# ScalarE copies a finished layer's rows straight into the PSUM factor, in place of the DMAs that spread them and one wide copy

## Chip, cores and metric

The kernel runs on one core of a Trainium2 chip. The metric is the device time of one execution in microseconds; less is better. TensorE (PE) multiplies, VectorE (DVE) forms products and remainders, ScalarE (ACT) rounds, copies and applies the activation, GpSimd (POOL) forms remainders, and SyncE's queue (SP) issues the DMAs.

## What is computed

A compressed interaction network over 512 samples with 32 fields and 16 embedding dimensions. Each of three layers multiplies every row of its input with every one of the 32 field rows and contracts the products with a weight matrix:

```python
def _cin(x0, conv_params, split_flags):
    B, _, D = x0.shape
    x = x0
    results = []
    for (W, b), split in zip(conv_params, split_flags):
        h = x.shape[1]
        z = jnp.einsum('bhd,bmd->bhmd', x, x0).reshape(B, h * x0.shape[1], D)
        xk = jax.nn.relu(jnp.einsum('oc,bcd->bod', W, z) + b[None, :, None])
        if split:
            half = xk.shape[1] // 2
            x, xk = (xk[:, :half], xk[:, half:])
        else:
            x = xk
        results.append(xk)
    return jnp.sum(jnp.concatenate(results, axis=1), axis=2)
pooled = _cin(sparse_embed, [(W1, b1), (W2, b2), (W3, b3)], [True, True, False])
return pooled @ Wo.T + bo
```

Each layer has 128 output rows. Layers 1 and 2 hand 64 of them on as the next layer's x; the other 64, and all of layer 3, are results. Everything is float32.

## The kernel before

**Tiling.** The 512 x 16 = 8192 columns are cut into 16 chunks of 512 columns. Layer 1 of a chunk is one group of 4 product tiles of 128 x 512 and a quarter tile; layers 2 and 3 are four groups of 4 tiles each. A pass i of the program works on layer 1 of chunk i (group 0 of the pass), layer 2 of chunk i-1 (groups 1 to 4) and layer 3 of chunk i-2 (groups 5 to 8), in this order on every engine. Passes run from 0 to 17; passes 0, 1, 16 and 17 hold fewer groups, and passes 4 to 13 are a loop. The first three groups (pass 0, and groups 0 and 1 of pass 1) are "native": no rounding, all matmuls in plain fp32.

**One group.** DVE multiplies a factor with the field rows and writes product tiles `z` (`product`, L533). ACT rounds them to `zh` (L423). POOL forms the remainder `zl` = `z` - `zh` (L481); in groups 0, 1, 3, 5 and 7 one tile goes another way: DVE writes it to PSUM (`zx_ps`), ACT rounds it (L427), and DVE subtracts (L594). PE multiplies `zh` (L682, L684, L690), the native tiles (L694), and last `zl` (L700, L706), into the layer's accumulator `y_ps`. Groups 2, 4, 6 and 8 give POOL three tiles (1536 columns), the others two (1024). The z buffers form a ring of three: a product waits until PE is through with the group three before (`group_used`).

**The factor.** In layers 2 and 3 the factor of a group is `a_ps[:, half, :]`, in PSUM: half 0 for the layer's first two groups, half 1 for the last two. It holds the 64 rows of the finished layer's x in blocks of 32 partitions: rows 0-31, 32-63, 0-31, 32-63 in half 0, and 32-63, 0-31, 32-63, 0-31 in half 1. ACT writes x to SBUF as `x_out[layer]` (L391, partitions 0-63 for layer 1 and 64-127 for layer 2), SP's queue copies it with five DMAs (`spread`, L323; two for half 0, three for half 1) into `a_rep`, and ACT copies each half, 128 x 512, to `a_ps` (`a_to_psum`, L378). The native group 1 of pass 1 reads `a_rep` itself.

**Order on ACT.** After the zh of a group ACT does other work written at that place in `body` (L414): at group 0 the copy for layer 2's half 1; at group 3 that for layer 3's half 0 and layer 3's result (`y_to_sbuf(3)`); at group 4 `y_to_sbuf(1)`, that is x (L391) and result (L399, partitions 64-127) of layer 1; at group 5 the copy for layer 3's half 1 and then `x_to_psum` (L375), the factor of the next pass's layer 1; at group 7 the copy for layer 2's half 0 and `y_to_sbuf(2)`. The queue is in order: a zh waits for what stands before it.

**Order on SP.** One queue issues all DMAs. In pass i: the spread of layer 1's x, once it exists; (pass 0) the rest of the first `b_fac`, the field rows that layers 2 and 3 multiply with, and the second part of layer 2's weights; (pass 1) layer 3's weights; the field rows of chunk i+2 (`load_x`, 1.5 MB); the spread of layer 2's x; `b_fac` of chunk i+1 (2 MB).

Of the kernel before, what the change touches and what calls it, by code (L numbers as in the profile page):

```python
# [44 lines left out]
P = 128  # L45
Q = 32
# [3 lines left out]
CH = 512  # L50
# [3 lines left out]
HALF = 64  # L54
# [85 lines left out]
def i_is(i, number):  # L140

    return isinstance(i, int) and i == number


def exists(chunk):

    return not isinstance(chunk, int) or 0 <= chunk < NCHUNK
# [36 lines left out]
def cin_kernel(nc, xt, w1, w2, w3, cols, bo, out):  # L184
    with ExitStack() as ctx:
        def sb(name, shape, dt=F32):
            return ctx.enter_context(nc.sbuf_tensor(name, shape, dt))

        def sem(name):
            return ctx.enter_context(nc.semaphore(name))  # L190
# [24 lines left out]
        x_out = {layer: sb(f"x{layer}_sb", [P, CH]) for layer in (1, 2)}  # L215
        results12 = sb("results12", [P, CH])
        results3 = sb("results3", [P, CH])
        a_rep = {2: sb("a2_rep", [P, 2, CH]), 3: sb("a3_rep", [P, 2, CH])}

        z_fifth = (results3, x_out[2])  # L220

# [6 lines left out]
        def psum(name, shape):  # L228
# [23 lines left out]
        b0_loaded = (sem("b0_loaded"), sem("b0_rest_loaded"))  # L252
        b_loaded = sem("b_loaded")
        x_in_psum = sem("x_in_psum")
        a_spread = {2: (sem("a2_0_spread"), sem("a2_1_spread")),
                    3: (sem("a3_0_spread"), sem("a3_1_spread"))}
        a_in_psum = {2: (sem("a2_0_in_psum"), sem("a2_1_in_psum")),
                     3: (sem("a3_0_in_psum"), sem("a3_1_in_psum"))}
        z_native_ready = sem("z_native_ready")
# [16 lines left out]
        out_ready = sem("out_ready")  # L276
        out_stored = sem("out_stored")
        LAST = (NCHUNK - 1) * ROWS * CH
        X_DMAS, B_DMAS, A_DMAS = 8, 4, (2, 3)

        def bank(layer, c):

            return y_ps[2] if layer == 3 and i_is(c, NCHUNK - 1) else y_ps[layer]
# [3 lines left out]
        @block.sync  # L287
        def _(sp):
            def rows_of(c, first, partitions, tiles):

                run = bass.AP(xt.tensor, first * CH, partitions + tiles[:-1] + [[1, LAST + tiles[-1][1]]])
                n = bass.ds(c * (ROWS * CH), tiles[-1][1])
                return run[:, n] if len(tiles) == 1 else run[:, :, n]

            def load_x(c):

                if not isinstance(c, int) or c > 1:
                    sp.wait_ge(x_loaded, (c - 1) * (16 * X_DMAS))

                place = (c % XSLOTS) * (XT * CH)  # L300
                loaded = x0_loaded if i_is(c, 0) else x_loaded
                for r in range(P // Q):
                    rows = slice(Q * r, Q * r + Q)
                    sp.dma_start(shifted[rows, bass.ds(place, GT * CH)],
                                 rows_of(c, GT * r, [[CH, Q]], [[1, GT * CH]])).then_inc(loaded, 16)
                    sp.dma_start(shifted[rows, bass.ds(place + XQ * CH, 2 * CH)].rearrange("p (t n) -> p t n", t=2),
                                 rows_of(c, Q // 2, [[CH, Q]], [[Q // 2 * CH, 2], [1, CH]])).then_inc(loaded, 16)

            def load_b(c, parts=None):

                if not isinstance(c, int) or c > 1:
                    sp.wait_ge(b_loaded, (c - 1) * (16 * B_DMAS))
                if not isinstance(c, int) or c >= BSLOTS:

                    sp.wait_ge(z_native_ready, groups_before(c))
                for j, end, loaded in parts or ((0, 8, b_loaded),):
                    size = (end - j) * CH
                    dst = b_fac[:, bass.ds((c % BSLOTS) * (8 * CH) + j * CH, size)]
                    for m in range(4):
                        sp.dma_start(dst[Q * m:Q * m + Q], rows_of(c, 8 * m + j, [[0, Q]], [[1, size]])  # L320
                                     ).then_inc(loaded, 16)

            def spread(layer, c):  # L323

                sp.wait_ge(x_ready[layer], c + 1)
                top = X_HALF[layer].start

                for k, to, rows, count in ((0, 0, 0, 2), (0, 2, 0, 2), (1, 1, 0, 2), (1, 3, 0, 1), (1, 0, 1, 1)):
                    sp.dma_start(a_rep[layer + 1][Q * to:Q * (to + count), k, :],  # L329
                                 x_out[layer][top + Q * rows:top + Q * (rows + count), :]  # L330
                                 ).then_inc(a_spread[layer + 1][k], 16)

            def load_w(layer, w, part):

                middle = nat[layer] + split_part(layer, 0).stop
                tiles = slice(0, middle) if part == 0 else slice(middle, GT * GROUPS[layer])
                sp.dma_start(w_raw[layer][:, tiles, :], w[:, tiles, :]).then_inc(w_loaded[layer][part], 16)

            load_x(0)
            sp.dma_start(w1_sb[:, 0:2 * NAT1], w1[:, 0:2 * NAT1]).then_inc(w1_loaded, 16)  # L340
            sp.dma_start(w1_sb[:, 2 * NAT1:], w1[:, 2 * NAT1:]).then_inc(w1_rest_loaded, 16)
            sp.dma_start(cols_sb[:], cols).then_inc(cols_loaded, 16)
            load_x(1)
            load_w(2, w2, 0)
            load_b(0, ((0, 4, b0_loaded[0]),))

            def body(i):
                if exists(i):
                    spread(1, i)
                if i_is(i, 0):  # L350
                    load_b(0, ((4, 8, b0_loaded[1]),))
                    load_w(2, w2, 1)
                if i_is(i, 1):
                    load_w(3, w3, 0)
                    load_w(3, w3, 1)
                if exists(i + 2):
                    load_x(i + 2)
                if exists(i - 1):
                    spread(2, i - 1)
                if exists(i + 1):  # L360
                    load_b(i + 1)
                if i_is(i, 0):
                    sp.dma_start(bo_sb[:], bo).then_inc(bo_loaded, 16)

            iterate(sp, body, NCHUNK)
            sp.wait_ge(out_ready, 2)
            sp.dma_start(out.rearrange("b o -> o b"), out_sb[:]).then_inc(out_stored, 16)
            sp.wait_ge(out_stored, 16)

        @block.scalar  # L370
        def _(act):
# [5 lines left out]

            def a_to_psum(layer, half, c):  # L378

                act.wait_ge(a_spread[layer][half], (c + 1) * (16 * A_DMAS[half]))  # L380
                nc.scalar.activation(a_ps[:, half, :], a_rep[layer][:, half, :], ACT.Copy  # L381
                                     ).then_inc(a_in_psum[layer][half], 1)

            def y_to_sbuf(layer, c):
                act.wait_ge(group_used, groups_through(layer, c))
                if i_is(c, 0) and layer == 1:
                    act.wait_ge(cols_loaded, 16)
                if layer < 3:

                    x = X_HALF[layer]  # L390
                    nc.scalar.activation(x_out[layer][x, :], bank(layer, c)[x, :], ACT.Relu,  # L391
                                         bias=cols_sb[x, layer - 1:layer]).then_inc(x_ready[layer], 1)
                results, rows = (results12, results12, results3)[layer - 1], RESULTS[layer]

                if layer == 2:
                    act.wait_ge(pooled12_done, c + 1)
                elif not isinstance(c, int) or c > 0:
                    act.wait_ge(pooled12_done if layer == 1 else pooled3_done, c)
                nc.scalar.activation(results[rows, :], bank(layer, c)[rows, :], ACT.Relu,  # L399
                                     bias=cols_sb[rows, layer - 1:layer]).then_inc(results_ready[layer], 1)  # L400

            def round_w(layer, part):
                if layer > 1:
                    act.wait_ge(w_loaded[layer][part], 16)
                tiles = split_part(layer, part)
                nc.scalar.activation(wh[layer][:, tiles, :], w_raw[layer][:, nat[layer]:, :][:, tiles, :], ACT.Copy
                                     ).then_inc(w_rounded[layer], 1)
# [6 lines left out]
            def body(i):  # L414
                here = {step[0]: (step, k) for k, step in enumerate(steps(i))}
                for pos in range(PER_ITER):
# [16 lines left out]
                    if pos == 0 and i_is(i, 0):  # L433
                        y_to_sbuf(1, 0)
                    if pos == 0 and i_is(i, 1):
                        round_w(2, 0)
                        a_to_psum(2, 0, 0)
                        a_to_psum(2, 1, 0)
                        round_w(2, 1)
                    if pos == 4 and i_is(i, 1):  # L440
# [47 lines left out]
        def _(dve):  # L488
# [44 lines left out]
            def product(i, step, k):  # L533
# [13 lines left out]
                else:  # L547
# [4 lines left out]
                        dve.wait_ge(b0_loaded[j], 16 * B_DMAS)  # L552
                    elif layer == 2 and g == 0:
                        dve.wait_ge(b_loaded, c * (16 * B_DMAS))
                    if is_native(q):
                        factor = a_rep[layer][:, half, :]
                        dve.wait_ge(a_spread[layer][half], 16 * A_DMAS[half])
                    else:
                        factor = a_ps[:, half, :]
                        dve.wait_ge(a_in_psum[layer][half], c + 1)  # L560
                if not isinstance(q, int) or q >= RING:
                    dve.wait_ge(group_used, q - (RING - 1))

# [203 lines left out]
```

## Time and profile before

| | us |
|---|---|
| median of 3 runs | 476.99 (476.26 to 477.19) |
| the profiled execution | 476.04 |
| its span in the trace | 474.3 |

| engine | busy us | share of the span |
|---|---|---|
| PE | 443.5 | 94% |
| DVE | 425.9 | 90% |
| POOL | 408.4 | 86% |
| ACT | 310.8 | 66% |

The DMA engines are over 90% busy for the first eighth of the span and 50 to 90% for most of the rest. The granted PE clock is full from the seventh of 40 slices on. How to read it: a row of a timeline has the start, the duration, the instruction, and in brackets how long the engine sat idle before it and for whom; neighbours of one kind are merged (x3). PE's matmuls are pipelined, so the spacing of their starts, not their duration, is what a matmul costs; the same holds for ACT where one instruction starts before the one before it has ended.

### The profile page before, as it was taken

The numbers are of one execution on the slowest core, as the hardware profiler recorded it, in microseconds if no ns is written. First come the engines' busy times: TensorE is split into PE (matmuls) and PEld (weight loads), VectorE is DVE, ScalarE is ACT, GpSimd is POOL, SyncE is SP. The second block draws the span as 40 slices with busy tenths as digits, with TensorE's granted clock in tenths as the row PEclk, the third lists the DMA queues.
The fourth block names the chain that finished last, engine by engine and source line by source line (L and its number), as shares of the span: only waits on it lengthen the run. The fifth ranks groups of instructions, "written<-read, shape, count | busy, mean of one in ns | idle before, by whom it ended". The sixth has DMA issues, their size and how long they took to land.

```text
span 474.3 us, 5975 instructions
## 1 busy us (share of the span) xinstructions
PE 443.5 (94%) x1601; PEld 302.2 (64%) x1601; DVE 425.9 (90%) x489; ACT 310.8 (66%) x383; POOL 408.4 (86%) x147
## 2 busy tenths in 40 slices
PE   0758499999999999999999999999999999999997
PEld 0325365676767767676766767666766767677774
DVE  1557599999999999999999999999999999999997
ACT  1224667685868767585868767685877768577661
POOL 0107399998999999999999999999999999899995
PEclk9988799999999999999999999999999999999999
DMA  8999999979595959879595968969495963922100
GB/s 211 242 234 228 248 229 211 224 171 228 117 228 119 224 121 215 172 162 214 124 230 110 222 133 193 205 138 238 103 229 119 225 144 69 198 44 46 25 19 1
DMA packets 23232, 78.42 MB, mean 165 GB/s; under 512 B 5939, under 2 KB 5939, under 8 KB 18996
## 3 DMA queue, kind: packets, MB, share of 16 engines
q1 hardware_dynamic: 23220, 78.28, 75.3%
q8 instruction: 5, 0.08, 0.1%
q14 instruction: 7, 0.06, 0.0%
HBM read 61.48 MB, written 0.00 MB: 130 GB/s over the span
## 4 chain that ended last, share of the span: by engine, by line
PE 84%; DMA 6%; DVE 4%; SPq 2%; ACT 1%; issue 1%; POOL 1%; DVEq 0%
PE y_ps L694 26%; PE y_ps L700 15%; PE y_ps L682 15%; PE y_ps L684 15%; PE y_ps L690 7%; PE y_ps L706 4%; DMA a_rep<-x_sb 3%; DVE z L530 3%; DMA w_raw<-w_dram 2%; DMA shifted<-xt_dram 1%; PE y_ps L660 1%; POOL zl L481 1%; SPq L329 1%; PE y_ps L686 1%; PE y_ps L702 1%
## 5 line engine op out<-in xcount | busy, mean ns | idle before, releaser
L481 POOL TENSOR_TENSOR zl<-z,zh 128x1024 fp32r<-128x1024 f32 (+1 forms) x141 | 406.6, 2920 | 48.6 <-ACT zh L423 48.3
L530 DVE TENSOR_TENSOR z<-a_ps,b_fac 128x1536 f32<-128x1536 f32 x254 | 269.7, 1083 | 24.4 <-PE y_ps L706 12.0
L423 ACT ACTIVATE zh<-z 128x1024 fp32r<-128x1024 f32 (+1 forms) x141 | 176.8, 1254 | 111.9 <-DVE z L530 111.5
L700 PE MATMUL y_ps<-zl,w_high 128*128 128x512 f32 x332 | 154.0, 557 | 2.3 <-POOL zl L481 2.3
L682 PE MATMUL y_ps<-zh,w_high 128*128 128x512 f32 x332 | 131.8, 397 | 8.4 <-ACT zh L423 8.4
L684 PE MATMUL y_ps<-zh,w_low 128*128 128x512 f32 x332 | 130.8, 394 | 0.0
L694 PE MATMUL y_ps<-z,w_raw 128*128 128x512 f32 x254 | 129.9, 593 | 0.0
L700 PEld LDWEIGHTS y_ps<-zl,w_high 128*128 128x128 f32 x332 | 62.2, 188 | 71.0 <-issue 61.1
L682 PEld LDWEIGHTS y_ps<-zh,w_high 128*128 128x128 f32 x332 | 62.7, 189 | 23.7 <-issue 6.4
L684 PEld LDWEIGHTS y_ps<-zh,w_low 128*128 128x128 f32 x332 | 63.0, 190 | 13.8
L694 PEld LDWEIGHTS y_ps<-z,w_raw 128*128 128x128 f32 x254 | 48.0, 189 | 10.6
L594 DVE TENSOR_TENSOR zl<-zx_ps,zh 128x512 fp32r<-128x512 f32 x77 | 52.3, 680 | 0.0
L381 ACT ACTIVATE a_ps<-a_rep 128x512 f32<-128x512 f32 x64 | 38.0, 594 | 16.3 <-DMA a_rep<-x_sb 16.3
L427 ACT ACTIVATE zh<-zx_ps 128x512 fp32r<-128x512 f32 x77 | 45.0, 585 | 0.4
L530 DVE TENSOR_TENSOR zx_ps<-a_ps,b_fac 128x512 f32<-128x512 f32 x63 | 43.3, 688 | 0.0
L399 ACT ACTIVATE results<-y_ps,cols_sb 64x512 f32<-64x512 f32 (+1 forms) x48 | 32.7, 682 | 6.0 <-PE y_ps L700 5.2
L530 DVE TENSOR_TENSOR z<-x_ps,shifted 128x1024 f32<-128x1024 f32 x28 | 34.1, 1218 | 2.3 <-PE y_ps L700 0.9
L706 PE MATMUL y_ps<-zl,w_high 128*128 128x512 f32 x77 | 30.5, 396 | 0.0
L690 PE MATMUL y_ps<-zh,w_low 128*128 128x512 f32 x77 | 30.4, 395 | 0.0
L690 PE MATMUL y_ps<-zh,w_high 128*128 128x512 f32 x77 | 30.3, 393 | 0.0
L694 PE MATMUL y_ps<-z,w_sum 128*128 128x512 f32 x56 | 26.7, 598 | 0.0
L391 ACT ACTIVATE x_sb<-y_ps,cols_sb 64x512 f32<-64x512 f32 x32 | 21.7, 677 | 4.6 <-PE y_ps L663 4.1
(45 smaller groups left out, 166.9 us busy)
## 6 DMA issues: line engine op xcount, KB each, us to landing
b_fac<-xt_dram SPq DMA_DIRECT2D x60, 512.0 KB, 8.9
shifted<-xt_dram SPq DMA_DIRECT2D x64, 256.0 KB, 4.9
a_rep<-x_sb SPq DMA_DIRECT2D x96, 128.0 KB, 3.1
shifted<-xt_dram SPq DMA_DIRECT2D x64, 128.0 KB, 5.2
a_rep<-x_sb SPq DMA_DIRECT2D x64, 64.0 KB, 2.6
b_fac<-xt_dram SPq DMA_DIRECT2D x8, 256.0 KB, 10.6
w_raw<-w_dram SPq DMA_DIRECT2D x2, 640.0 KB, 13.0
w_raw<-w_dram SPq DMA_DIRECT2D x2, 384.0 KB, 12.3
```

What stands on the lines that cost most here:

```text
L381: nc.scalar.activation(a_ps[:, half, :], a_rep[layer][:, half, :], ACT.Copy).then_inc(a_in_psum[layer][half], 1)
L423: nc.scalar.activation(zh[:, slot, 0:end - native, :], z[:, slot, native:end, :], ACT.Copy).then_inc(zh_ready, 1)
L427: nc.scalar.activation(zh[:, slot, end - native, :], zx_ps[:, ZX_BANK[pos], :], ACT.Copy).then_inc(zxh_ready, 1)
L481: nc.gpsimd.tensor_tensor(zl[:, slot, 0:end - native, :], z[:, slot, native:end, :], zh[:, slot, 0:end - native, :].bitcast(F32), ALU.subtract
L530: return nc.vector.tensor_tensor(dst, factor.unsqueeze(1).to_broadcast(list(dst.shape)), others, ALU.mult)
L594: nc.vector.tensor_tensor(zl[:, slot, end - native, :], zx_ps[:, ZX_BANK[pos], :], zh[:, slot, end - native, :].bitcast(F32), ALU.subtract ...
L682: nc.tensor.matmul(y, wh[layer][:, w, :], zh[:, slot, t, :], start=(g == 0 and t == 0), stop=False)
L684: nc.tensor.matmul(y, wl[layer][:, w, :], zh[:, slot, t, :], start=False, stop=False)
L690: nc.tensor.matmul(y, weights[layer][:, x_weights, :], zh[:, slot, x_part, :], start=False, stop=False)
L694: nc.tensor.matmul(y, w_raw[layer][:, natives.index((g, t)), :], z[:, slot, t, :], start=False, stop=False)
L700: mm = nc.tensor.matmul(y, wh[layer][:, w, :], zl[:, slot, t, :], start=False, stop=end_here)
L706: mm = nc.tensor.matmul(y, wh[layer][:, x_weights, :], zl[:, slot, x_part, :], start=False, stop=last)
```

## The change

`spread`, `a_rep`, its semaphores and the 5 DMAs per layer and chunk (160 in all) are gone. `a_to_psum` waits for `x_ready` and copies from `x_out` into the partition blocks of `a_ps`: half 0 with two copies of 64 rows, half 1 with four of 32. Its places in ACT's order are the same, but for the first one in pass 1, which moves ahead of `round_w(2, 0)`. `y_to_sbuf` of layers 1 and 2 gets two waits, so that x isn't overwritten before its copies are done. `load_x` waits for `x_ready[1]`. The native group reads `a_ps` as all others do.

```diff
@@ sync: load_x
                 if not isinstance(c, int) or c > 1:
                     sp.wait_ge(x_loaded, (c - 1) * (16 * X_DMAS))
+                    sp.wait_ge(x_ready[1], c - 1)
@@ sync
-            def spread(layer, c):
-                sp.wait_ge(x_ready[layer], c + 1)
-                top = X_HALF[layer].start
-                for k, to, rows, count in ((0, 0, 0, 2), (0, 2, 0, 2), (1, 1, 0, 2), (1, 3, 0, 1), (1, 0, 1, 1)):
-                    sp.dma_start(a_rep[layer + 1][Q * to:Q * (to + count), k, :],
-                                 x_out[layer][top + Q * rows:top + Q * (rows + count), :]
-                                 ).then_inc(a_spread[layer + 1][k], 16)
@@ sync: body
-                if exists(i):
-                    spread(1, i)
...
-                if exists(i - 1):
-                    spread(2, i - 1)
@@ scalar
             def a_to_psum(layer, half, c):
-                act.wait_ge(a_spread[layer][half], (c + 1) * (16 * A_DMAS[half]))
-                nc.scalar.activation(a_ps[:, half, :], a_rep[layer][:, half, :], ACT.Copy
-                                     ).then_inc(a_in_psum[layer][half], 1)
+                act.wait_ge(x_ready[layer - 1], c + 1)
+                top, size = X_HALF[layer - 1].start, (HALF, Q)[half]
+                for to, row in (((0, 0), (HALF, 0)), ((Q, 0), (2 * Q, Q), (3 * Q, 0), (0, Q)))[half]:
+                    copy = nc.scalar.activation(a_ps[to:to + size, half, :],
+                                                x_out[layer - 1][top + row:top + row + size, :], ACT.Copy)
+                copy.then_inc(a_in_psum[layer][half], 1)
@@ scalar: y_to_sbuf
                 if layer < 3:
                     x = X_HALF[layer]
+                    if not isinstance(c, int) or c > 0:
+                        for half in range(2):
+                            act.wait_ge(a_in_psum[layer + 1][half], c)
@@ scalar: body
                     if pos == 0 and i_is(i, 1):
+                        a_to_psum(2, 0, 0)
                         round_w(2, 0)
-                        a_to_psum(2, 0, 0)
                         a_to_psum(2, 1, 0)
@@ vector: product
-                    if is_native(q):
-                        factor = a_rep[layer][:, half, :]
-                        dve.wait_ge(a_spread[layer][half], 16 * A_DMAS[half])
-                    else:
-                        factor = a_ps[:, half, :]
-                        dve.wait_ge(a_in_psum[layer][half], c + 1)
+                    factor = a_ps[:, half, :]
+                    dve.wait_ge(a_in_psum[layer][half], c + 1)
```

## Rows read from the trace of the kernel before

**Rows 1.** Windows: busy us per engine (x instructions), granted clock, DMA share, GB/s.

```profile
274.57:301.50 26.93, 26.93 (x101) 18.79 (x101) 25.82 (x31) 19.40 (x24) 25.77 (x10) 1.00 0.80 173
```

**Rows 2.** Waits of the whole run: waiter <- releaser, total us, times, longest.

```profile
ACT a_ps L381 <- DMA a_rep<-x_sb: 16.3, 4, 8.8
PE y_ps L682 <- ACT zh L423: 8.4, 2, 6.0
PE y_ps L700 <- POOL zl L481: 2.3, 3, 1.1
```

**Rows 3.** The chain that ended last, up to 80 us: start us, us, what.

```profile
37.28 14.70 DMA a_rep<-x_sb
...
52.69 1.23 DVE z L530
...
74.53 3.50 POOL zl L481
```

**Rows 4.** DMA issues and their landing: the last b_fac piece issued at 11.47, and at 29.85.

```profile
b_fac<-xt_dram SPq DMA_DIRECT2D x1, 256.0 KB, 14.4
...
b_fac<-xt_dram SPq DMA_DIRECT2D x1, 512.0 KB, 21.1
```

**Rows 5.** Timeline of ACT: a copy early in pass 1, the zh of group 6 in pass 2.

```profile
27.97 0.60 ACT L381 ACTIVATE a_ps<-a_rep 128x512 f32<-128x512 f32 x1 [0.50 <-DMA a_rep<-x_sb]
...
72.97 1.49 ACT L423 ACTIVATE zh<-z 128x1536 fp32r<-128x1536 f32 x1 [1.34 <-DVE z L530]
```

**Rows 6.** Timeline of ACT, pass 10, groups 4 to 6.

```profile
281.72 1.49 ACT L423 ACTIVATE zh<-z 128x1536 fp32r<-128x1536 f32 x1 [0.73 <-DVE z L530]
283.12 0.66 ACT L391 ACTIVATE x_sb<-y_ps,cols_sb 64x512 f32<-64x512 f32 x1
283.80 0.68 ACT L399 ACTIVATE results<-y_ps,cols_sb 64x512 f32<-64x512 f32 x1
284.51 1.06 ACT L423 ACTIVATE zh<-z 128x1024 fp32r<-128x1024 f32 x1
285.60 0.60 ACT L427 ACTIVATE zh<-zx_ps 128x512 fp32r<-128x512 f32 x1
286.09 0.60 ACT L381 ACTIVATE a_ps<-a_rep 128x512 f32<-128x512 f32 x1
286.61 0.59 ACT L375 ACTIVATE x_ps<-shifted 128x512 f32 x1
287.76 1.49 ACT L423 ACTIVATE zh<-z 128x1536 fp32r<-128x1536 f32 x1 [0.55 <-DVE z L530]
```

**Rows 7.** Timeline of DVE, pass 10, groups 4 and 7.

```profile
279.93 2.35 DVE L530 TENSOR_TENSOR z<-a_ps,b_fac 128x1536 f32<-128x1536 f32 x2 [0.42 <-PE y_ps L706]
...
288.84 1.21 DVE L530 TENSOR_TENSOR z<-a_ps,b_fac 128x1024 f32<-128x1024 f32 x1
```

**Rows 8.** Timeline of POOL, group 6 of pass 10.

```profile
289.33 3.52 POOL L481 TENSOR_TENSOR zl<-z,zh 128x1536 fp32r<-128x1536 f32 x1
```

**Rows 9.** Timeline of PE: a stall in pass 2, then group 6 of pass 10.

```profile
78.07 0.96 PE L700 MATMUL y_ps<-zl,w_high 128*128 128x512 f32 x3 [1.05 <-POOL zl L481]
78.87 0.39 PE L682 MATMUL y_ps<-zh,w_high 128*128 128x512 f32 x1
...
292.80 1.02 PE L694 MATMUL y_ps<-z,w_raw 128*128 128x512 f32 x2
294.34 0.40 PE L682 MATMUL y_ps<-zh,w_high 128*128 128x512 f32 x1
```

**Rows 10.** Waits within pass 10 (274.57 to 301.50): total us, times, longest.

```profile
ACT zh L423 <- DVE z L530: 7.4, 7, 2.5
```

**Rows 11.** Timeline of ACT, last pass: both halves, group 6.

```profile
452.93 0.58 ACT L381 ACTIVATE a_ps<-a_rep 128x512 f32<-128x512 f32 x1
...
456.25 0.59 ACT L381 ACTIVATE a_ps<-a_rep 128x512 f32<-128x512 f32 x1
457.67 1.49 ACT L423 ACTIVATE zh<-z 128x1536 fp32r<-128x1536 f32 x1 [0.82 <-DVE z L530]
```

More of the change, by code:

```diff
@@ L217, in cin_kernel @@
         results3 = sb("results3", [P, CH])
-        a_rep = {2: sb("a2_rep", [P, 2, CH]), 3: sb("a3_rep", [P, 2, CH])}
         z_fifth = (results3, x_out[2])
@@ L254, in cin_kernel @@
         x_in_psum = sem("x_in_psum")
-        a_spread = {2: (sem("a2_0_spread"), sem("a2_1_spread")),
-                    3: (sem("a3_0_spread"), sem("a3_1_spread"))}
         a_in_psum = {2: (sem("a2_0_in_psum"), sem("a2_1_in_psum")),
@@ L278, in cin_kernel @@
         LAST = (NCHUNK - 1) * ROWS * CH
-        X_DMAS, B_DMAS, A_DMAS = 8, 4, (2, 3)
+        X_DMAS, B_DMAS = 8, 4
         def bank(layer, c):
```

## The prediction

> **What bounds the kernel now.** I read the windows first. [...] The waits come next: ACT waits for the spread's DMAs in only 4 copies, and PE for zh twice and for zl three times in the whole run [rows 2]. All of that lies in the startup: in the steady part the spread's latency is hidden, and its removal is worth nothing there. The chain of waits shows where it counts: a spread issued at 37.28 lands 14.70 us later, the product of group 1 of pass 2 starts at 52.69, DVE's chain goes on to POOL's remainder of group 6 at 74.53, and PE stalls for it at 78.07 [rows 3, 9]. From there PE runs without a gap to the end. The kernel's time is therefore the point at which PE gets going plus what each later pass takes.
>
> The change touches both: it takes DMAs out of the startup and puts eight more ACT instructions into every pass (12 copies in place of 4).
>
> **Startup, first term.** The second spread needed 14.70 us because it queued behind other loads. As ACT copies, issued when x is ready, it is out of the way. What is late next is `b_fac` of chunk 1, which group 1 of pass 2 multiplies with: its last piece, issued at 29.85, lands 21.1 later, at 50.95 [rows 4]. It in turn moves earlier by the first spread, which stood ahead of it in the queue. The last piece of the first `b_fac` landed at 11.47 + 14.4 = 25.87 [rows 4], the spread's second half at 27.97 [rows 5]: 2.1 us of queue time. So `b_fac` lands at about 48.85 and the product starts there instead of at 52.69: 3.8 us gained. SP no longer stops for x before the rest of `b_fac` and layer 2's weights, but the DMA engines are full in this stretch, so order, not issue time, counts. `load_x`'s new wait is for an x that was awaited before too, and layer 3's weights, now ahead of chunk 3's field rows, delay nothing that is due soon. Bounds for this term: 1.7 (if `b_fac` doesn't move) and 6 (if it lands some 2 us earlier still).
>
> **What one copy costs.** No copy of 32 or 64 rows stands in the trace, so I bound it. A copy of 128 x 512 takes 0.60 [rows 6]. Rows don't matter: x and result of 64 partitions take 0.66 and 0.68, the same as wide ones of their kind. What matters is when the next instruction starts. `a_ps` starts 0.11 before the end of the one before it, and `x_ps` follows at a spacing of 0.52. But the layer's result, on partitions 64 to 127, starts 0.02 after x's end, on 0 to 63; the zh behind it 0.03 after that one's end; and the next instruction, the first to read PSUM from partition 0 again, 0.03 after the zh's end [rows 6]. An instruction whose operands start at other partitions than the last ones in that memory seems to wait until the one before it has ended. Each of the new copies changes the block that it reads or writes, except the very first of a layer 2 half 0. I take 0.60 + 0.02 = 0.62 each; the lower bound is 0.52, the upper 0.71, the spacing of result and zh.
>
> [...]
>
> **Steady passes, second term: group 5.** Eight more copies make ACT 19.4 + 8 x 0.6 = about 24 busy of 26.9; as a sum this fits. In place it doesn't at group 5, where four copies and `x_to_psum` stand before the zh of group 6. The path: DVE's product of group 4 waits for PE's end of group 1 and starts at 279.93 [rows 7]; its zh 281.72, x, result, zh of group 5 at 284.51 (no idle time before it, so its product was ready), zx rounded until 286.20 [rows 6]. All this is ACT without a pause. Now four copies from 286.22 at 0.62 reach 288.70, `x_ps` (another start partition again) ends at 289.30, and the zh of group 6 starts at 289.21 rather than 287.76: 1.45 late. POOL's remainder started at 289.33 [rows 8], 0.08 behind that zh's end (287.76 + 1.49), so it comes 1.45 late too: 290.78, end 290.78 + 3.52 = 294.30.
>
> What does PE feel of it? In the stall of pass 2 POOL ended at 74.53 + 3.48 = 78.01 and PE began the next group at 78.87 [rows 9]: 0.86 later. In pass 10 the group after begins at 294.34 [rows 9], so POOL may end at 293.48; it ended at 292.85, a margin of 0.63. The loss is 1.45 - 0.63 = 0.82. Two copies at group 3 push the zh of group 4 by about 0.03: 0.85 per pass. PE can't win it back, because the path begins at PE's own end of group 1. It counts in passes 3 to 14: 12 x 0.85 = 10.2 us. In pass 15 `x_to_psum` is missing, so the zh starts 0.5 earlier: 0.3.
>
> **Steady passes, the other places.** Two copies at group 3: the product of group 4 is ready at 281.7, and ACT has sat idle for 0.73 before its zh [rows 6], enough for the copy (0.62) with the lost overlaps: 0.03, counted above. ACT waits 7 times in a pass for DVE, 7.4 us in all and up to 2.5 at once [rows 10]; only group 5 and what follows it have little of that. At group 7 one copy more (0.62, and 0.5 for a later start) makes the zh of group 8 about 1.1 late, while POOL comes to it 1.45 late itself. At group 0 three copies more delay the zh of group 1 by some 1.2 at most less the idle time before it, and POOL is again behind by its own 1.45. The product of group 7 at 288.84 [rows 7] needs the four copies, done at 288.68: just in time, and DVE has 1 us per pass in hand. The two new waits of `y_to_sbuf` are for copies done long before. None of this adds.
>
> **Pass 2 and the last pass.** In pass 2 the copies at group 5 push the zh of group 6 as well, but ACT had been idle for 1.34 before it rather than 0.55 [rows 5, 6]: 1.45 - 0.79 = 0.7 late, and PE starts its gapless run that much later. In the last pass group 5's product waits for `a_ps`: two copies from 452.93, 0.12 + 0.62 = 0.75 late; then four copies where one stood at 456.25, until 457.13 + 2.48 = 459.61, and the zh of group 6 at 459.63 rather than 457.67 [rows 11]. That is 1.95 less the margin of 0.63: 1.3.
>
> **The sum.** -3.8 + 0.7 + 10.2 + 0.3 + 1.3 = +8.7. On the profiled execution, 476.04 (span 474.3 and 1.7 around it), this gives 484.7. That execution is 0.95 below the median of 476.99, so the median to expect is 485.7.
>
> **Rival A: the copies overlap as `a_ps` and `x_ps` do, 0.52 apart.** Then the zh of group 6 is late by 3 x 0.52 - 0.63 (idle time and overlap) = 0.93, and a pass loses 0.30: 3.6 in 12. With 0.2 in pass 2 and 0.6 in the last, -3.8 + 0.2 + 3.6 + 0.6 = +0.6: 477.6. For it: rows with one start partition. Against it: the three gaps in rows 6.
>
> [...]
>
> **Rival B, faster: a copy of 32 rows is cheap.** The place is the same, ACT between the groups 5 and 6. With spacing s a pass loses 4s - 1.63; at s = 0.41 it loses nothing and the startup's gain stays whole: -3.7, so 473.3. The two sides balance at about s = 0.48. Only a cost that falls with the rows could give that, and x and result at 64 rows show no such fall.
>
> **Rival C, slower still: 0.71 per copy**, as behind the result. Four copies at 0.09 more in 14 passes: +5, so 490.7. Also here: the four copies would end at 289.06, after the product of group 7 wants them.
>
> **How the numbers follow.** The forecast's case has 0.65, with 482 to 489 by the bounds of the startup term. A has 0.13, B 0.09, C 0.13. The range leaves out B, half of A's lower side and the top of C: 477 to 491. A measurement of this kernel can tell about 0.2%, 1 us, from no change. Slower by more: the forecast, C and a bit of A, 0.81. Within: most of A, 0.08. Faster: B and a long startup gain with A, 0.11.
>
> **What would show it.** The first product of group 1 in pass 2 near 48.9; copies 0.62 apart; in a steady pass a PE wait of about 0.6 to 0.85 at L700 of group 6 on POOL, a pass of 27.8 instead of 26.93, and ACT near 24 busy. If PE is still busy throughout, the spacing or the margin is wrong; if it stalls at other groups too, I missed a place. If the product starts near 51, `b_fac` doesn't move with the queue.

## The result, and the profile after

The changed kernel takes 483.38 us (median of 4 runs, 483.06 to 484.04) against 476.72 (476.26 to 477.19): a ratio of 1.014 (95% interval 1.0127 to 1.0153), 6.7 us slower (the median of the kernel before is now that of four runs, hence not 476.99). The forecast was 485.7, slower.

The page of the changed kernel, part 1:

```profile
span 481.5 us, 5947 instructions
PE 446.9 (93%) x1601; PEld 299.3 (62%) x1601; DVE 426.9 (89%) x489; ACT 389.2 (81%) x511; POOL 408.0 (85%) x147
```

ACT has 128 more instructions and 78 us more busy time (310.8 before), 0.61 each; no other engine has more instructions. Yet PE, with the same 1601 matmuls, needs 7.2 us more of span. In this kernel's code zh is L413, the copies L367, x and result L381 and L389, the product L520, zl L471, and PE's last matmuls of a group L686 and L692.

Its waits, whole run (waiter <- releaser, total, times, longest):

```profile
POOL zl L471 <- ACT zh L413: 56.9, 33, 20.6
ACT zh L413 <- DVE z L520: 49.1, 49, 1.9
DVE z L520 <- DMA b_fac<-xt_dram: 10.1, 3, 5.8
PE y_ps L686 <- POOL zl L471: 10.0, 16, 1.1
```

The waits for the spread [rows 2] are gone, and DVE waits for `b_fac` instead. PE waits for POOL 16 times where it did 3 times. Where, the timeline of PE shows (idle time in brackets):

```profile
74.53 0.97 PE L686 MATMUL y_ps<-zl,w_high 128*128 128x512 f32 x3 [1.05 <-POOL zl L471]
102.30 0.97 PE L686 MATMUL y_ps<-zl,w_high 128*128 128x512 f32 x3 [0.54 <-POOL zl L471]
...
268.48 0.97 PE L686 MATMUL y_ps<-zl,w_high 128*128 128x512 f32 x3 [0.47 <-POOL zl L471]
...
296.18 0.97 PE L686 MATMUL y_ps<-zl,w_high 128*128 128x512 f32 x3 [0.47 <-POOL zl L471]
296.98 0.39 PE L668 MATMUL y_ps<-zh,w_high 128*128 128x512 f32 x1
...
407.00 0.97 PE L686 MATMUL y_ps<-zl,w_high 128*128 128x512 f32 x3 [0.55 <-POOL zl L471]
...
470.72 0.97 PE L686 MATMUL y_ps<-zl,w_high 128*128 128x512 f32 x3 [1.05 <-POOL zl L471]
```

The stall at 74.53 is that at 78.07 [rows 9]: the startup is 3.54 us shorter. From 102.30 to 407.00, in passes 3 to 14, there is one stall per pass, always before the last matmuls of group 6, and a pass takes 27.70 (268.48 to 296.18) instead of 26.93. Passes 15 and 16 list none, and the last stall lies in pass 17. The idle time in brackets, 0.47, is less than the 0.77 that a pass loses: it counts from the modelled end of the matmul before, and the three matmuls behind the stall then follow one another closer than before (296.18 to 296.98, 0.80; in the kernel before 293.25 to 294.34, 1.09). I go by the length of the pass.

ACT in pass 10, groups 4 to 6, the place of [rows 6]:

```profile
283.61 1.48 ACT L413 ACTIVATE zh<-z 128x1536 fp32r<-128x1536 f32 x1
284.99 0.67 ACT L381 ACTIVATE x_sb<-y_ps,cols_sb 64x512 f32<-64x512 f32 x1
285.69 0.68 ACT L389 ACTIVATE results<-y_ps,cols_sb 64x512 f32<-64x512 f32 x1
286.39 1.06 ACT L413 ACTIVATE zh<-z 128x1024 fp32r<-128x1024 f32 x1
287.48 0.60 ACT L417 ACTIVATE zh<-zx_ps 128x512 fp32r<-128x512 f32 x1
288.10 2.40 ACT L367 ACTIVATE a_ps<-x_sb 32x512 f32<-32x512 f32 x4
290.53 0.60 ACT L359 ACTIVATE x_ps<-shifted 128x512 f32 x1
291.07 2.42 ACT L413 ACTIVATE zh<-z 128x1536 fp32r<-128x1536 f32 x2
```

No idle time stands in any of these rows. The four copies take 2.43 from 288.10 to the start of the next instruction, 0.61 each. From the product of group 4 the zh of group 6 is 9.26 away (281.81 to 291.07); before it was 7.83 (279.93 to 287.76) [rows 6, 7]: 1.43 more. The product of DVE and the remainder of POOL at these places:

```profile
281.81 2.35 DVE L520 TENSOR_TENSOR z<-a_ps,b_fac 128x1536 f32<-128x1536 f32 x2 [0.42 <-PE y_ps L692]
...
292.62 3.50 POOL L471 TENSOR_TENSOR zl<-z,zh 128x1536 fp32r<-128x1536 f32 x1 [1.42 <-ACT zh L413]
```

POOL now sits idle for 1.42 us before group 6, ends at 296.12, and PE begins the next group at 296.98, 0.86 later.

**Where the 7 us come from.** The startup gives -3.54. The twelve stalls of passes 3 to 14 cost +9.3: from 74.53 to 407.00 are 332.47, and 12 x 26.93 would be 323.16. The last activation, behind the matmuls of the last group, starts at 477.69; before:

```profile
470.14 0.69 ACT L399 ACTIVATE results<-y_ps,cols_sb 128x512 f32<-128x512 f32 x1 [5.21 <-PE y_ps L700]
```

That is +7.55, so passes 15 to 17 hold the remaining 1.8 (7.55 + 3.54 - 9.3). The last matmuls of single groups place it, each time in the changed kernel and in the one before: PE is 5.74 behind at group 7 of pass 14 (409.66 and 403.92), 6.05 at group 7 of pass 15 (436.89 and 430.84), still 6.06 at group 5 of pass 17 (466.14 and 460.08) and 7.44 at group 7 of pass 17 (473.36 and 465.92), behind the last stall. The span grew by 7.2; what lies behind that activation is 0.35 shorter, which I didn't pursue.

### The profile page after: what moved, and what is told of

It reads as the page before. It is cut to its first block, busy times and chain, and to the rows that moved or that the text cites. A ratio compares the mean times of both kernels' runs of the same rounds, so it can differ in the third digit from the quotient of the medians.

```text
span 481.5 us, 5947 instructions
## 1 busy us (share of the span) xinstructions
PE 446.9 (93%) x1601; PEld 299.3 (62%) x1601; DVE 426.9 (89%) x489; ACT 389.2 (81%) x511; POOL 408.0 (85%) x147
## 4 chain that ended last, share of the span: by engine, by line
POOL 34%; issue 22%; PE 16%; DMA 11%; DVE 9%; ACT 4%; SPq 3%; POOLq 0%; DVEq 0%
POOL zl L471 34%; DMA b_fac<-xt_dram 6%; DVE z L520 5%; DMA shifted<-xt_dram 5%; PE y_ps L680 5%; PE y_ps L686 3%; PE y_ps L668 3%; PE y_ps L670 3%; ACT zh L413 1%; SPq L302 1%; PE y_ps L676 1%; SPq L304 1%; ACT a_ps L367 1%; DVE terms L510 1%; DVE zl L580 1%
## 5 line engine op out<-in xcount | busy, mean ns | idle before, releaser
L471 POOL TENSOR_TENSOR zl<-z,zh 128x1024 fp32r<-128x1024 f32 (+1 forms) x141 | 406.3, 2922 | 56.9 <-ACT zh L413 56.9
L520 DVE TENSOR_TENSOR z<-a_ps,b_fac 128x512 f32<-128x512 f32 (+2 forms) x256 | 272.3, 1086 | 25.1 <-PE y_ps L692 11.9
L413 ACT ACTIVATE zh<-z 128x1024 fp32r<-128x1024 f32 (+1 forms) x141 | 175.0, 1250 | 50.0 <-DVE z L520 49.1
L686 PE MATMUL y_ps<-zl,w_high 128*128 128x512 f32 x332 | 146.0, 533 | 10.0 <-POOL zl L471 10.0
L367 ACT ACTIVATE a_ps<-x_sb 32x512 f32<-32x512 f32 (+1 forms) x192 | 113.9, 593 | 2.7
L686 PEld LDWEIGHTS y_ps<-zl,w_high 128*128 128x128 f32 x332 | 60.5, 190 | 85.3 <-issue 41.8
L520 DVE TENSOR_TENSOR z<-x_ps,shifted 128x1024 f32<-128x1024 f32 x28 | 34.2, 1220 | 12.3 <-PE y_ps L686 11.8
L520 DVE TENSOR_TENSOR zx_ps<-a_ps,b_fac 128x512 f32<-128x512 f32 x63 | 43.4, 690 | 0.0
L389 ACT ACTIVATE results<-y_ps,cols_sb 64x512 f32<-64x512 f32 (+1 forms) x48 | 32.8, 684 | 7.1 <-PE y_ps L686 5.9
L692 PE MATMUL y_ps<-zl,w_high 128*128 128x512 f32 x77 | 30.7, 399 | 2.6 <-DVE zl L580 2.6
L381 ACT ACTIVATE x_sb<-y_ps,cols_sb 64x512 f32<-64x512 f32 x32 | 21.6, 675 | 7.3 <-PE y_ps L649 4.4
```

The source lines that it names most:

```text
L367: copy = nc.scalar.activation(a_ps[to:to + size, half, :], x_out[layer - 1][top + row:top + row + size, :], ACT.Copy)
L413: nc.scalar.activation(zh[:, slot, 0:end - native, :], z[:, slot, native:end, :], ACT.Copy).then_inc(zh_ready, 1)
L471: nc.gpsimd.tensor_tensor(zl[:, slot, 0:end - native, :], z[:, slot, native:end, :], zh[:, slot, 0:end - native, :].bitcast(F32), ALU.subtract
L520: return nc.vector.tensor_tensor(dst, factor.unsqueeze(1).to_broadcast(list(dst.shape)), others, ALU.mult)
L686: mm = nc.tensor.matmul(y, wh[layer][:, w, :], zl[:, slot, t, :], start=False, stop=end_here)
```

## Experiments

Two theories stood against each other. **Place**: the loss arises in ACT's queue between the zh of group 5 and that of group 6, and the gain in the startup; each other copy is free. **Load**: ACT at 24 us of 27 per pass is too full, wherever the copies stand.

**e1: copies in the startup only.**

```diff
+COPIED = {(2, 0): (0, 2), (2, 1): (0, 2), (3, 0): (0, 1), (3, 1): (0, 1)}
```

The table gives, for each layer and half, the chunks that are filled by copies; all others go by the spread and one wide copy. Of the edit only the table is shown, here and in e2 and e3: the rest brings `spread`, `a_rep` and their semaphores back beside the copies.

> Copies from x only for chunks 0 and 1 of layer 2 and chunk 0 of layer 3 (the startup); from then on the DMAs and one wide copy, as before. Place theory (the loss arises in ACT's queue between groups 5 and 6 of the steady passes, the gain in the startup): 476.7 - 3.5 = 473.2, PE's last stall near 74.5 and a steady pass of 26.93. Rival (the startup's gain is an artefact of the later passes, or the DMAs that stay take it back): 476 to 477.

Measured: 472.48 (472.27 to 472.60), ratio 0.9914 (0.989 to 0.9937). The last stall of PE before its gapless run:

```profile
74.85 0.96 PE L724 MATMUL y_ps<-zl,w_high 128*128 128x512 f32 x3 [1.05 <-POOL zl L509]
```

The median is 0.7 below the 473.2 expected. So the startup's gain (the span goes from 474.3 to 470.7) is real and stands by itself; the DMAs that stay take nothing back.

**e2: all by copies except layer 3's half 1.**

```diff
+COPIED = {(2, 0): (0, 99), (2, 1): (0, 99), (3, 0): (0, 99), (3, 1): (0, 0)}
```

> All copies from x except layer 3's half 1 (group 5), which stays a DMA spread and one wide copy. ACT has 9 copies per pass instead of 12. Place theory: no loss in a steady pass (26.93) and the startup's gain: 473 to 474. Load theory (the loss goes with ACT's busy time, whatever the place): 5 of the 8 extra copies stay, so 5/8 of some 10 us remain: 479.5.

Measured: 472.35 (471.91 to 472.77), ratio 0.9911 (0.9887 to 0.9936): 0.65 below the lower end of what the place theory expected.

**e3: only layer 3's half 1 by copies.**

```diff
+COPIED = {(2, 0): (0, 0), (2, 1): (0, 0), (3, 0): (0, 0), (3, 1): (0, 99)}
```

As in the kernel before, `round_w(2, 0)` stands ahead of the first `a_to_psum` of pass 1 here.

> Only layer 3's half 1 (group 5) as four copies from x; all else by DMA, as before. ACT has 7 copies per pass. Place theory: the full loss per pass of the changed kernel (27.70) without the startup's gain: about 487. Load theory: 3/8 of the loss: 480.5.

Measured: 487.21 (median of 5, from 487.06; one run at 490.25), ratio 1.0225 (1.0201 to 1.0249). The trace is that of the run at 490.25, whose granted clock in the fifth of the 40 slices is only 0.5, against 0.7 in the kernel before; so I read nothing of its startup, and of the rest only a pass at a clock of 1.00. Windows of one pass, first e2, then e3 (busy us of PE, PEld, DVE, ACT, POOL, each with its instructions; clock, DMA share, GB/s):

```profile
280.00:306.93 26.93, 26.93 (x101) 18.80 (x101) 25.83 (x31) 22.65 (x30) 25.78 (x10) 1.00 0.70 146
```

```profile
276.16:303.86 27.70, 27.21 (x101) 18.67 (x101) 25.79 (x31) 21.14 (x28) 25.73 (x10) 1.00 0.77 164
```

This pair settles it. In e2 ACT is busy for 22.65 per pass and PE doesn't pause in it; in e3 it is busy for only 21.14 and the pass takes 27.70, exactly that of the changed kernel. The load theory expected 479.5 and 480.5 and falls; five more copies at the groups 0, 3 and 7 are free, three more at group 5 cost it all.

**e4: the copy of x to PSUM moved behind group 6.**

```diff
-if pos == (3 if i_is(i, 1) else 5) and exists(i + 1) and not i_is(i, 0):
+if pos == (3 if i_is(i, 1) else 6) and exists(i + 1) and not i_is(i, 0):
     x_to_psum(i + 1)
```

> The changed kernel with the copy of x to PSUM moved from behind group 5 to behind group 6: as many instructions on ACT, one fewer between the copies and the zh of group 6. Place theory: that zh starts 0.54 earlier, a pass loses 0.23 instead of 0.77, 12 passes give 6.5 us back: 477. Load theory: unchanged, 483.4.

Measured: 477.17 (476.22 to 477.43), ratio 1.0009 (0.9999 to 1.0019), 6.2 less than the changed kernel. ACT behind group 5, and the zh of group 6 a pass later:

```profile
284.74 2.41 ACT L367 ACTIVATE a_ps<-x_sb 32x512 f32<-32x512 f32 x4
287.17 1.49 ACT L413 ACTIVATE zh<-z 128x1536 fp32r<-128x1536 f32 x1
288.56 0.58 ACT L359 ACTIVATE x_ps<-shifted 128x512 f32 x1
...
314.34 1.49 ACT L413 ACTIVATE zh<-z 128x1536 fp32r<-128x1536 f32 x1
```

A pass of 27.17: the loss is 0.24 where 0.23 was expected. The same instructions, one of them moved by a few places, give 0.53 per pass back. It also checks the margin: from the product of group 4, at 278.45, the zh of group 6 is 8.72 away instead of 9.26, and 0.54 less delay at the zh is 0.53 less at PE.

**e5: four copies that all start at partition 0.**

```diff
+if (layer, half) == (3, 1):
+    source = w_raw[2][:, 0:GT, :].rearrange("p t n -> p (t n)")
+    for k in range(4):
+        target = scratch[:, k, :] if k < 3 else a_ps[:, half, :]
+        copy = nc.scalar.activation(target, source, ACT.Copy)
...
```

> The changed kernel, but layer 3's half 1 is filled by four copies of 128 rows that all start at partition 0, from layer 2's weights (three to a scratch tile, the last to the factor), so layer 3's last two groups get a factor that isn't x. As many instructions of as many columns, no change of start partition. Hold theory (an instruction that starts at other partitions than the last waits for its end): spacing 0.52 instead of 0.61, the zh of group 6 starts 0.5 earlier, a pass of 27.2 instead of 27.70, 477 in all. Rival (an ACT instruction of 512 columns takes 0.6 in a row whatever its partitions): unchanged, 483.4.

Measured: 478.50 (478.29 to 478.58), 4.9 less than the changed kernel. ACT behind group 5:

```profile
285.12 0.60 ACT L425 ACTIVATE zh<-zx_ps 128x512 fp32r<-128x512 f32 x1
285.62 1.66 ACT L371 ACTIVATE scratch<-w_raw 128x512 f32<-128x512 f32 x3
287.29 0.60 ACT L371 ACTIVATE a_ps<-w_raw 128x512 f32<-128x512 f32 x1
287.82 0.59 ACT L360 ACTIVATE x_ps<-shifted 128x512 f32 x1
288.35 2.42 ACT L421 ACTIVATE zh<-z 128x1536 fp32r<-128x1536 f32 x2
315.65 2.42 ACT L421 ACTIVATE zh<-z 128x1536 fp32r<-128x1536 f32 x2
```

The durations of the three merged copies (shortest, median, longest, in ns):

```profile
L371 ACT ACTIVATE scratch<-w_raw x3: 617/621/621, 285.6 to 286.7; 128x512 f32<-128x512 f32 x3
```

Each copy starts before the one before it has ended (0.10 before the end of L425; the three take 1.66 together and 0.62 each, so they are 0.52 apart, as expected), except the last: it starts 0.01 after its predecessor's end (285.62 + 1.66 = 287.28). It is the first to write PSUM again, at partition 0, and the last write to PSUM, behind group 3, began at partition 64. So the one copy that I had not meant to be held is held, for the very reason of the theory. Its hold accounts for the pass of 27.30 (288.35 to 315.65) instead of 27.2: it starts 0.11 later than at the spacing of the others. 12 x 0.1 is most of the 1.5 us by which the total missed. The rival, 483.4, falls.

e5 changed more than the start partitions: its copies have 128 rows, and three of them write SBUF. The trace of the changed kernel has a pair without these differences. The first copy of a half 0 has the same 64 rows, the same target and the same neighbour in front of it in both layers; only its source starts at partition 64 for layer 3 (first pair) and at partition 0 for layer 2 (second pair):

```profile
281.19 0.58 ACT L417 ACTIVATE zh<-zx_ps 128x512 fp32r<-128x512 f32 x1
281.80 1.20 ACT L367 ACTIVATE a_ps<-x_sb 64x512 f32<-64x512 f32 x2
...
293.39 0.57 ACT L417 ACTIVATE zh<-zx_ps 128x512 fp32r<-128x512 f32 x1
293.87 1.19 ACT L367 ACTIVATE a_ps<-x_sb 64x512 f32<-64x512 f32 x2
```

The first starts 0.03 behind its predecessor's end, the second 0.09 ahead of it. So the start partition holds a copy back, and not the number of its rows.

**e6: e2 with chunk 1's `b_fac` in two halves.**

```diff
-load_b(i + 1)
+load_b(i + 1, ((0, 4, b1_loaded), (4, 8, b_loaded)) if i_is(i, 0) else None)
...
+elif layer == 2 and i_is(c, 1):
+    if g == 0:
+        dve.wait_ge(b1_loaded, 16 * B_DMAS)
+    elif g == 1:
+        dve.wait_ge(b_loaded, 16 * B_DMAS)
```

> The kernel with all copies from x but group 5's, and chunk 1's b_fac loaded in two halves of 4 tiles with a semaphore each, so that group 1 of pass 2 waits for the first half alone. Theory (b_fac is what is late next in the startup): group 1's product starts near 44.2 instead of 48.9; group 2's then waits for the four copies that fill half 1, to about 50.0 instead of 51.9: 1.9 gained, 470.5. Rival (the chain through ACT and PE of pass 1 binds as well): 472.3, no change.

Measured: 470.70 (470.17 to 470.77), ratio 0.9873 (0.9857 to 0.989): the fastest of all, 1.65 below e2. DVE's products of groups 1 and 2 in pass 2, and ACT's next zh:

```profile
43.75 1.23 DVE L559 TENSOR_TENSOR z<-a_ps,b_fac 128x1024 f32<-128x1024 f32 x1 [1.11 <-DMA b_fac<-xt_dram]
...
48.38 2.35 DVE L559 TENSOR_TENSOR z<-a_ps,b_fac 128x1536 f32<-128x1536 f32 x2 [1.61 <-DMA b_fac<-xt_dram]
```

```profile
47.10 2.41 ACT L406 ACTIVATE a_ps<-x_sb 32x512 f32<-32x512 f32 x4
49.53 1.06 ACT L452 ACTIVATE zh<-z 128x1024 fp32r<-128x1024 f32 x1
```

The total came as expected, the way only in part: group 2's product reads half 0, not half 1 as I had written, and waits for the second half of `b_fac`. The product of group 2 starts 3.45 earlier than in e2 (51.83 there). What stops the gain at 1.7 instead of 3.5 is the zh of group 1, which stands behind the four copies until 49.53, though its product was ready at 45 (43.75 + 1.23). How that reaches the end, POOL and DVE show, in e2 and then in e6:

```profile
51.29 2.38 POOL L509 TENSOR_TENSOR zl<-z,zh 128x1024 fp32r<-128x1024 f32 x1 [4.22 <-ACT zh L451]
55.17 6.60 POOL L509 TENSOR_TENSOR zl<-z,zh 128x1536 fp32r<-128x1536 f32 x2 [1.51 <-ACT zh L451]
...
57.61 1.89 DVE L520 TENSOR_TENSOR w_low<-w_raw,w_high 128x768 fp32r<-128x768 f32 x1
```

```profile
50.67 8.94 POOL L510 TENSOR_TENSOR zl<-z,zh 128x1024 fp32r<-128x1024 f32 x3 [3.68 <-ACT zh L452]
...
54.64 2.70 DVE L521 TENSOR_TENSOR w_low<-w_raw,w_high 128x768 fp32r<-128x768 f32 x1
```

POOL's remainder of group 1, behind that zh, starts only 0.62 earlier than in e2; that of group 2 then follows without idle time, at 53.02 instead of 55.17, and ends 2.16 earlier. DVE comes to the remainder of layer 3's weights (`w_low`) 2.97 earlier, but leaves it only 2.15 earlier (57.34 instead of 59.49), 0.8 behind the end of POOL's remainder in both kernels. PE's stalls at group 6 of pass 2 (71.70 and 73.86) differ by 2.16 as well, the spans by 2.1, the medians by 1.65. Here, too, copies ahead of a zh are the limit; that without them the whole 3.5 would arrive wasn't tried.

**e7: the first spread back on the DMA queue.**

```diff
-COPIED = {(2, 0): (0, 2), (2, 1): (0, 2), (3, 0): (0, 1), (3, 1): (0, 1)}
+COPIED = {(2, 0): (1, 2), (2, 1): (1, 2), (3, 0): (0, 1), (3, 1): (0, 1)}
...
-a_to_psum(2, 0, 0)
 round_w(2, 0)
+a_to_psum(2, 0, 0)
```

Here e7 is shown against e1.

> The start-only kernel, but layer 2's chunk 0 by the DMA spread as before; only chunk 1 (and layer 3's chunk 0) by copies. Queue theory (the first spread delays b_fac by its 2.1 us of queue time): the product of group 1 in pass 2 starts at 51.0 instead of 48.9: 472.5 + 2.1 = 474.6. Rival (b_fac lands when it lands, only the second spread's own wait counted): 472.5.

Measured: 474.72 (474.44 to 474.82), ratio 0.9955 (0.9938 to 0.9972), 2.24 above e1. The product of group 1 in pass 2, in e7 and in e1:

```profile
51.54 1.23 DVE L558 TENSOR_TENSOR z<-a_ps,b_fac 128x1024 f32<-128x1024 f32 x1 [6.18 <-DMA b_fac<-xt_dram]
```

```profile
49.28 1.23 DVE L558 TENSOR_TENSOR z<-a_ps,b_fac 128x1024 f32<-128x1024 f32 x1 [6.17 <-DMA b_fac<-xt_dram]
```

2.26 apart: the startup's gain has the two parts of the prediction, the second spread's own wait and the first spread's place in the queue ahead of `b_fac`. e7 also puts two other things back as they were: ACT's order early in pass 1, which isn't in this path, as DVE waits over 6 us for `b_fac` in both kernels, and SP's stop for x ahead of the later loads. SP begins to issue chunk 1's `b_fac` at 28.55 in e7 and at 23.24 in e1. Of these 5.3 us only 2.26 appear at the landing, so the issue time alone doesn't set it; the stop and the five DMAs weren't tried one without the other.

## Why the prediction held, step by step

**Startup, -3.8 and +0.7.** `b_fac` was forecast at 48.85. In the changed kernel:

```profile
48.96 1.22 DVE L520 TENSOR_TENSOR z<-a_ps,b_fac 128x1024 f32<-128x1024 f32 x1 [5.81 <-DMA b_fac<-xt_dram]
```

3.7 earlier than at 52.69 [rows 3], and what is late next is what was named; e7 shows the queue's part of it. At the start of PE's run, at group 6 of pass 2, 3.54 are left, not 3.1. The copies cost there nearly what was forecast, 0.63 for 0.7: DVE's product for group 6 starts at 67.03, the zh behind the copies at 69.44, 2.41 later, where it was 1.78 (71.19 to 72.97) with ACT waiting for DVE. But DVE came to it 0.4 earlier than by the shift alone, because the first remainder of layer 3's weights took less; the kernel before, then the changed one:

```profile
61.41 2.29 DVE L492 TENSOR_TENSOR w_low<-w_raw,w_high 128x768 fp32r<-128x768 f32 x1
...
71.19 2.34 DVE L530 TENSOR_TENSOR z<-a_ps,b_fac 128x1536 f32<-128x1536 f32 x2
```

```profile
57.67 1.88 DVE L482 TENSOR_TENSOR w_low<-w_raw,w_high 128x768 fp32r<-128x768 f32 x1
...
67.03 2.34 DVE L520 TENSOR_TENSOR z<-a_ps,b_fac 128x1536 f32<-128x1536 f32 x2
```

The sum had taken that instruction as unchanged. The traces show what its length goes with: it takes 0.95 while POOL is idle, but the two of layer 3 start while POOL forms a remainder, and they end 0.81 to 0.82 behind the end of that remainder in all nine traces, after 1.19 to 3.42 us. In the changed kernel POOL's remainder ends 4.15 earlier (58.73 instead of 62.88), and `w_low` 4.16. So DVE gets as far ahead as POOL does there, and not only by the 3.7 of `b_fac`. No run varied it by itself.

**One copy, 0.62.** It took 0.61, and ACT is busy for 24.3 per pass, as forecast. That the hold, and not the rows, sets it, was an inference from three gaps in [rows 6]; e5 shows it, with a spacing of 0.52 at one start partition and the held copy standing out by itself, and so does the pair of 64-row copies beside it.

**Group 5, 0.85 per pass.** It is 0.77: the zh comes 1.43 later, not 1.48, POOL starts 1.41 later, and the margin is 0.64 rather than 0.63. The sign named for it, an idle time of 0.6 to 0.85 before PE's last matmuls, came out as 0.47; the length of a pass, which the sum used, shows the loss. The 0.03 for group 3's copies was too much: from its product the zh of group 4 is as far as before (281.81 to 283.61, 1.80; before 279.93 to 281.72, 1.79). Twelve passes make this the largest error of the sum, 0.9.

**The other places, nothing.** e2 shows it: with nine copies and the four of group 0 among them PE is busy in each of 26.93 us, at a granted clock of 1.00. PE sets the pace of that pass, as in [rows 1]; DVE (25.83) and POOL (25.78) are 1.10 and 1.15 below it.

**Passes 15 to 17, +1.6.** 1.8 came, and the shifts of PE above show where: 0.3 in pass 15, as forecast, and 1.4 at the stall of pass 17, for 1.3; 0.1 more lies behind it. No experiment tested these two.

**The sum.** +8.7 was forecast for the span, +7.2 came; on the medians +6.7. The three errors (0.4 in the startup, 0.9 in the steady passes, 0.35 behind the last activation) all go the same way, less 0.2 in the last passes. The path and the place held, and each term to within 1 us. The direction came out right by no luck: the loss in the steady passes is more than twice the startup's gain, and e1 and e3 show the two apart.

**The rivals.** A (copies 0.52 apart, 477.6) had the right mechanism for the wrong operands: e5 comes to 478.5. B needed copies that get cheaper with fewer rows; 32 rows take 0.59 to 0.60, as 128 do. C's 0.09 more per copy did not come.

## What to carry to other kernels

An engine with a quarter of its time free can still set the pace (ACT in e3, busy for 21.14 of 27.70): add up what stands in its queue between two instructions that others wait for, not its busy time, and look for the margin that the next engines have there. If a latency hurts only in the startup, take it away only there (e1), or keep the old form at the one place without room (e2). The narrow ACT copies here cost as much as the wide ones (0.59 to 0.60 at 32 rows in e3, 0.58 to 0.60 at 128 in the kernel before), and stood a little further apart where each started at another partition (0.61 in the changed kernel, 0.52 in e5).

## What the runs showed of the hardware

- An ACT copy of 512 columns to PSUM takes 0.58 to 0.60 whether it has 128 rows (the kernel before, 64 copies) or 32 or 64 (the changed kernel, 192 copies); e5's copies of 128 rows to SBUF take 0.62 to 0.63 (48 of them, 615 to 627 ns).
- Behind an instruction with the same start partitions an ACT instruction starts 0.06 to 0.11 before its predecessor's end; where its source or target starts at another partition than the last one used in that memory, it starts 0.01 to 0.03 after the end. Those are the gaps in pass 10 of the kernel before [rows 6] and of the changed one, and in the pass shown of e4 and e5; e5's four copies and the pair of 64-row copies show both.
- VectorE's remainder of weights (two inputs from SBUF, 128x768) takes 0.95 to 0.96 while POOL is idle (18 times in nine traces). Started while POOL forms a remainder, it ends 0.81 to 0.82 behind that one's end, 18 times out of 18 in nine traces, at lengths from 1.19 to 3.42 (both in e3). The products that DVE forms while POOL forms a remainder don't stretch (2.34 to 2.36 for two of 1536 columns in [rows 7] and in the changed kernel).
